# First attention stage: the weights in memory with all heads of a token and key side by side, and pairs of heads 8 apart

## The reference

```python
disp = (x @ w_disp + b_disp)            # 16 heads of 16
val  = (x @ w_val + b_val)              # 16 heads of 16
val_win = windows(val, 32)              # for each token the 32 tokens that end with it
logits = bond(disp windows) - 10 * damage(disp windows)   # two GELUs of [b, head, t, 32, 16]
weights = softmax(where(cmask, logits, -inf), axis=-1)    # over the 32 keys
out = einsum('bntd,bntde->bnte', weights, val_win)
return out.transpose(0, 2, 1, 3).reshape(B, T, C) @ w_cproj + b_cproj
```

## Time and profile before

| | |
|---|---|
| median of three runs | 3115.01 us |
| lowest and highest | 3107.58 and 3115.89 us |
| the profiled execution | 3107.8 us |
| its span, first to last instruction | 3106.1 us |
| mean granted TensorE clock | 0.951 |
| busy in the span: PE, DVE, ACT, POOL | 91%, 54%, 50%, 42% |
| first attention, some 600 to 1330 us, in the stretch 820 to 880: PE, DVE, ACT, POOL busy | 53.1, 49.8, 53.4, 50.1 of 60 us |

### The profile page before, as it was taken

The page is one execution under the profiler, slowest core; times in us unless marked ns, Lnnn a source line. Parts: engine busy times, 40 slices in busy tenths (PEclk is TensorE's granted clock), DMA queues, the critical chain, the costliest instruction groups (busy, mean ns, idle before and its releaser), DMA issues. The chain is left out here.

```text
span 3106.1 us, 54232 instructions
## 1 busy us (share of the span) xinstructions
PE 2824.6 (91%) x19419; PEld 2032.8 (65%) x19419; DVE 1674.6 (54%) x4656; ACT 1556.4 (50%) x2621; POOL 1317.7 (42%) x1315
## 2 busy tenths in 40 slices
PE   6899999877898988588999998999879999998999
PEld 5799999732444443368999996666546566655676
DVE  5411111288888888363111112677776666666666
ACT  1133333369899898311333332333257777783333
POOL 5444444379888888163444442000043443320000
PEclk9899999889999999768999998999989999999999
DMA  8299999705566555862999997000052333301000
GB/s 288 73 327 328 325 329 325 224 16 37 59 60 65 56 62 62 97 201 86 326 325 328 328 326 228 5 1 1 25 133 72 78 98 94 91 1 39 14 14 20
DMA packets 360543, 432.23 MB, mean 139 GB/s; under 512 B 86721, under 2 KB 315238, under 8 KB 357222
## 3 DMA queue, kind: packets, MB, share of 16 engines
q1 hardware_dynamic: 334902, 394.66, 48.0%
q0 software_dynamic: 24576, 33.57, 5.1%
q10 hardware_dynamic: 816, 0.79, 0.1%
HBM read 356.08 MB, written 72.88 MB: 138 GB/s over the span
## 5 line engine op out<-in xcount | busy, mean ns | idle before, releaser
L1806 ACT ACTIVATE f_h_t<-f_h_ps,f_b_t 128x128 f32<-128x128 f32 x1024 | 319.6, 363 | 596.3 <-PE f_h_ps L1764 596.0
L2186 POOL TENSOR_TENSOR a_dmg_buf<-a_c 128x2048 f32<-128x2048 f32 x128 | 519.9, 4096 | 77.8 <-PE a_dmg_ps L2250 48.4
L1764 PEld LDWEIGHTS f_h_ps<-f_rows_t,f_w 128*128 128x128 f32 x4096 | 482.8, 194 | 9.9 <-issue 3.5
L1764 PE MATMUL f_h_ps<-f_rows_t,f_w 128*128 128x128 f32 x4096 | 483.9, 277 | 2.3 <-DVE f_rows_t L1820 1.2
L1778 PE MATMUL f_y_ps<-f_w,f_h_t 128*128 128x256 f32 x2048 | 483.4, 379 | 0.0
L1724 POOL DMA_INDIRECT acc_rows<-f_y,f_give x128 | 205.0, 1602 | 487.6 <-DMA acc_rows<-f_y,f_give 441.1
L1778 PEld LDWEIGHTS f_y_ps<-f_w,f_h_t 128*128 128x128 f32 x2048 | 369.8, 190 | 39.9
L1820 DVE COPY f_rows_t<-f_t_ps 128x256 f32<-128x256 f32 x128 | 54.3, 424 | 597.9 <-PE f_t_ps L1752 597.9
L2562 DVE SCALAR_TENSOR_TENSOR a_bond_buf<-a_a,a_small_rep,a_q_ps 128x512 f32<-128x512 f32 x512 | 346.6, 739 | 8.0 <-PE a_q_ps L2380 4.2
L999 ACT ACTIVATE a_prob<-a_prob,a_neg_top 128x384 f32<-128x384 f32 (+3 forms) x512 | 276.5, 570 | 46.7 <-POOL a_neg_top L816 46.5
L536 DVE SCALAR_TENSOR_TENSOR x_resid<-f_y_ps,f_gate,x_resid 128x256 f32 x512 | 216.7, 478 | 122.5 <-PE f_y_ps L384 111.9
(11 more groups left out here) (358 smaller groups left out, 4135.4 us busy)
## 6 DMA issues: line engine op xcount, KB each, us to landing
f_w<-in_L_ffn_w_dram SPq DMA_DIRECT2D x256, 1024.0 KB
a_skewed<-skew SPq DMA_DIRECT2D x32, 512.0 KB, 6.8
a_k_s<-parts SPq DMA_DIRECT2D x16, 768.0 KB, 7.8
acc_rows<-x_resid SPq DMA_DIRECT2D x17, 512.0 KB, 7.8
xn_rows<-f_xn SPq DMA_DIRECT2D x16, 512.0 KB, 3.6
a_vals<-val_rows SPq DMA_DIRECT2D x64, 128.0 KB, 3.9
skew<-a_bond SPq DMA_DIRECT2D x128, 64.0 KB
x_resid<-acc_rows SPq DMA_DIRECT2D x30, 256.0 KB, 7.0
```

The lines of the kernel that those rows point to most:

```text
L1764: last = nc.tensor.matmul(h_ps[n // HB][:, (n % HB) * P:(n % HB + 1) * P], w1_sb[s][:, c, n * P:(n + 1) * P], rows_t[e % 2][:, c, :], star ...
L1806: nc.scalar.activation(h_t[k][:, n, :], h_ps[n // HB][:, (n % HB) * P:(n % HB + 1) * P], ACT.Gelu, bias=b1_t[:, n, e:e + 1]).then_inc(gelu ...
L2186: nc.gpsimd.tensor_tensor(dmg_buf[n % RING][:, :, :], places(c_sb[h], first_place(dg)), c_sb[h][:, PAD:].unsqueeze(1).broadcast_to([P, DG, ...
```

## The change

The weights of a token are kept with the head as the innermost axis: `bond` becomes [128, 4 tiles, 32 keys, 16 heads], and `skew` and `skewed` are keys x heads as well. A token's 512 weights of a tile are then one run of 2 KB in SBUF and in DRAM, and a row is shifted by one key, 16 elements, against the row before. The 16 stores and 4 loads stay as they are in number and bytes. `copy_logits` writes in the new order, `find_top` and `inverse_sums` reduce over an axis whose elements are 16 apart, `less_top` subtracts along the middle axis. A block for `turn_weights` is now every eighth column, `skewed[:, x, hp::8]`, which holds heads hp and hp + 8, alternating, for 64 keys. So `vals` has its two halves on alternating partitions, the sums go to two places 128 columns apart in the result, and the values come out of their product in their natural order: `w_val` and `b_val` are used unsorted, and the copy of the bias to `b_val_r` goes.

```diff
--- before.py
+++ after.py
@@ -1892,7 +1892,7 @@
         sb = lambda n, s, dt=FP32: ctx.enter_context(nc.sbuf_tensor(f"{name}_{n}", s, dt))
         ps = lambda n, s: ctx.enter_context(nc.psum_tensor(f"{name}_{n}", s, FP32))
         sem = lambda n: core.semaphore(f"{name}_{n}")
-        w_val_sb = sb("w_val", [P, DC, HP, 2, BD])
+        w_val_sb = sb("w_val", [P, DC, D])
         w_out_sb = sb("w_out", [P, DC, D])
 
         b_out_sb = sb("b_out", [3, D])
@@ -1901,8 +1901,7 @@
         ones = sb("ones", [3, P], BF16)
         w_disp_sb = sb("w_disp", [P, DC, D])
         b_disp_r = sb("b_disp", [P, D])
-        b_val_sb = sb("b_val", [P, HP, 2, BD])
-        b_val_r = sb("b_val_r", [P, 2, HP, BD])
+        b_val_sb = sb("b_val", [P, D])
         bond_b = sb("bond_b", [P, 1])
         damage_b = sb("damage_b", [P, 1])
 
@@ -1948,8 +1947,9 @@
         dmg_buf = [sb(f"dmg_buf{k}", [P, DG, S]) for k in range(RING)]
         tanh = sb("tanh", [P, S])
         logits = sb("logits", [P, S])
-        bond = [sb(f"bond{k}", [P, TPB, NH, WIN]) for k in range(2)]
-        top = sb("top", [P, TPB * NH, 1])
+
+        bond = [sb(f"bond{k}", [P, TPB, WIN, NH]) for k in range(2)]
+        top = sb("top", [P, TPB, NH])
         inv_sum = [sb(f"inv_sum{k}", [P, TPB, NH]) for k in range(2)]
         skewed = sb("skewed", [P, TPB, NH * SPAN])
         turned = sb("turned", [P, HP, P])
@@ -2088,8 +2088,8 @@
                 sp.dma_start(dst, src, **kind).then_inc(loaded, 16)
             sp.dma_start(w_disp_sb[:, :, :], w_disp.rearrange("(c p) n -> p c n", p=P)).then_inc(disp_loaded, 16)
             load(b_disp_r[:, :], b_disp.partition_broadcast(P))
-            load(w_val_sb[:, :, :, :, :].rearrange("p c h r d -> p c (h r d)"), w_val.rearrange("(c p) n -> p c n", p=P))
-            load(b_val_sb[:, :, :, :].rearrange("p h r d -> p (h r d)"), b_val.partition_broadcast(P))
+            load(w_val_sb[:, :, :], w_val.rearrange("(c p) n -> p c n", p=P))
+            load(b_val_sb[:, :], b_val.partition_broadcast(P))
             load(bond_b[:, :], b_bond.partition_broadcast(P))
             load(damage_b[:, :], b_damage_out.partition_broadcast(P))
             load(w_out_sb[:, :, :], w_cproj.rearrange("(c p) n -> p c n", p=P))
@@ -2106,9 +2106,10 @@
                     if j:
                         sp.wait_ge(skew_loaded[x], j * 16)
                     for a in range(BPT):
-                        rows = bass.AP(tensor=skew_dram.tensor, offset=a * WIN * row + x * NH * SPAN + 1,
-                                       ap=[[row + 1, WIN], [SPAN, NH], [1, WIN]])
-                        sp.dma_start(rows, bond[j % 2][a * WIN:(a + 1) * WIN, x, :, :]).then_inc(skew_stored[x], 16)
+                        rows = bass.AP(tensor=skew_dram.tensor, offset=a * WIN * row + x * NH * SPAN + NH,
+                                       ap=[[row + NH, WIN], [1, WIN * NH]])
+                        sp.dma_start(rows, bond[j % 2][a * WIN:(a + 1) * WIN, x, :, :].rearrange("p w h -> p (w h)")
+                                     ).then_inc(skew_stored[x], 16)
                 for x in range(TPB):
                     if j:
                         sp.wait_ge(w_turned, (j - 1) * TPB + x + 1)
@@ -2135,7 +2136,7 @@
                 for r in range(2):
                     first = val_dram[S - WIN + x * P:, r * HP * BD:]
                     blocks = bass.AP(tensor=first.tensor, offset=first.offset, ap=[[D, SPAN], [WIN * D, BPT], [1, HP * BD]])
-                    sp.dma_start(vals[r * SPAN:(r + 1) * SPAN, x * BPT:(x + 1) * BPT, r, :], blocks).then_inc(val_loaded[x], 16)
+                    sp.dma_start(vals[r:2 * SPAN:2, x * BPT:(x + 1) * BPT, r, :], blocks).then_inc(val_loaded[x], 16)
 
             sp.wait_ge(core.cleared, 16 * core.clears)
             store_values(0)
@@ -2190,9 +2191,9 @@
             def less_top(j):
                 for n, tiles in enumerate(soft_parts(j)):
                     count = tiles.stop - tiles.start
-                    rows = bond[j % 2][:, tiles, :, :].rearrange("p j h w -> p (j h) w")
+                    rows = bond[j % 2][:, tiles, :, :]
                     pool.wait_ge(top_ready, j + n + 1)
-                    nc.gpsimd.tensor_tensor(rows, rows, top[:, tiles.start * NH:tiles.stop * NH, :].broadcast_to([P, count * NH, WIN]),
+                    nc.gpsimd.tensor_tensor(rows, rows, top[:, tiles, :].unsqueeze(2).broadcast_to([P, count, WIN, NH]),
                                             ALU.subtract).then_inc(soft_ready, 1)
 
             def split_bias():
@@ -2274,7 +2275,7 @@
                 for hp in range(HP):
                     bank = (t_ps, second(m))[hp // 4]
                     last = nc.tensor.transpose(bank[:, hp % 4 * P:(hp % 4 + 1) * P],
-                                               skewed[:, x, hp * P:(hp + 1) * P], core.ident[:, :])
+                                               skewed[:, x, hp:NH * SPAN:HP], core.ident[:, :])
                 last.then_inc(w_turned, 1)
 
             def sums(m):
@@ -2288,7 +2289,7 @@
                     pe.wait_ge(ctx_ready, m)
                 for hp in range(HP):
                     for a in range(BPT):
-                        last = nc.tensor.matmul(o_ps[a * WIN:(a + 1) * WIN, hp * 2 * BD:(hp + 1) * 2 * BD],
+                        last = nc.tensor.matmul(o_ps[a * WIN:(a + 1) * WIN, 0:D].rearrange("p (r h d) -> p h r d", r=2, d=BD)[:, hp, :, :],
                                                 turned[:, hp, a * WIN:(a + 1) * WIN],
                                                 vals[:, x * BPT + a, :, hp * BD:(hp + 1) * BD],
                                                 start=True, stop=True)
@@ -2308,7 +2309,7 @@
                     at = PAD + (2 * pair + j) * P
                     for c in range(DC):
                         last = nc.tensor.matmul(t_ps[:, j * D:(j + 1) * D], xn_t[i % NX][:, c, at:at + P],
-                                                w_val_sb[:, c, :, :, :].rearrange("p h r d -> p r h d"),
+                                                w_val_sb[:, c, :],
                                                 start=c == 0, stop=c == DC - 1)
                 last.then_inc(val_ready, 1)
 
@@ -2578,14 +2579,14 @@
 
                 j, part = divmod(g, GROUPS)
                 h, at = part // 2, slice(part % 2 * PG, (part % 2 + 1) * PG)
-                turned_g = bond_ps[g % 2][:, :].rearrange("p (j d h) -> p j h d", j=TPB, d=PG)
-                dst = bond[j % 2][:, :, h * HH:(h + 1) * HH, at]
+                turned_g = bond_ps[g % 2][:, :].rearrange("p (j d h) -> p j d h", j=TPB, d=PG)
+                dst = bond[j % 2][:, :, at, h * HH:(h + 1) * HH]
                 dve.wait_ge(logits_turned, g + 1)
                 if part == 0 and j >= 2:
                     for stored in skew_stored:
                         dve.wait_ge(stored, (j - 1) * 16 * BPT)
                 nc.vector.scalar_tensor_tensor(out=dst[:, 0, :, :], in0=turned_g[:, 0, :, :], scalar=bond_b[:, 0:1],
-                                               in1=early[:, at].unsqueeze(1).broadcast_to([P, HH, PG]),
+                                               in1=early[:, at].unsqueeze(2).broadcast_to([P, PG, HH]),
                                                op0=ALU.add, op1=ALU.add)
                 nc.vector.tensor_scalar(dst[:, 1:, :, :], turned_g[:, 1:, :, :], bond_b[:, 0:1], None,
                                         ALU.add).then_inc(logits_copied, 1)
@@ -2595,14 +2596,13 @@
                     dve.wait_ge(soft_ready, j)
                 nc.vector.drain()
                 for tiles in soft_parts(j):
-                    nc.vector.tensor_reduce(top[:, tiles.start * NH:tiles.stop * NH, 0],
-                                            bond[j % 2][:, tiles, :, :].rearrange("p j h w -> p (j h) w"),
+                    nc.vector.tensor_reduce(top[:, tiles, :], bond[j % 2][:, tiles, :, :].rearrange("p j w h -> p j h w"),
                                             AX.X, ALU.max).then_inc(top_ready, 1)
 
             def inverse_sums(j):
                 dve.wait_ge(exp_done, j + len(soft_parts(j)))
-                nc.vector.tensor_reduce(inv_sum[j % 2][:, :, :].rearrange("p j h -> p (j h)"),
-                                        bond[j % 2][:, :, :, :].rearrange("p j h w -> p (j h) w"), AX.X, ALU.add)
+                nc.vector.tensor_reduce(inv_sum[j % 2][:, :, :], bond[j % 2][:, :, :, :].rearrange("p j w h -> p j h w"),
+                                        AX.X, ALU.add)
                 nc.vector.drain()
                 nc.vector.reciprocal(inv_sum[j % 2][:, :, :], inv_sum[j % 2][:, :, :])
 
@@ -2631,7 +2631,7 @@
                 nc.vector.tensor_tensor(
                     val_rows[:, 2 * pair:2 * pair + 2, :, :].rearrange("p j r n -> p j (r n)"),
                     t_ps[:, :].rearrange("p (j n) -> p j n", j=2),
-                    b_val_r[:, :, :, :].rearrange("p r h d -> p (r h d)").unsqueeze(1).broadcast_to([P, 2, D]),
```

(2 more changed lines are left out.)

## The result

| kernel | median us | span of the profiled execution |
|---|---|---|
| before, 5 runs (3100.4 to 3115.9) | 3107.58 | 3106.1 |
| changed, 5 runs (3079.9 to 3082.4) | 3081.56 | 3078.1 |

The ratio is 0.992, with a 95% interval from 0.9899 to 0.9941: some 26 us faster. In a later session the same two kernels stood at 0.9947 (0.9930 to 0.9964), 16 us.

A forecast was written before the change was run, and what follows sets the result against it. No single bound for the program; in the first attention stage ScalarE sets the pace outside the ends. Gains of 27.9 us less 5.3 (reductions) and 5.9 (weight loads) leave 16.7, so 3115.0 becomes 3098.3 us, range 3083 to 3120.

The forecast's parts named there:

- a faster transfer brings nothing: Batches 1 to 5: ScalarE waits 1.57 and 0.72 us at two tiles with the load already in; zero gain claimed.
- nothing that shows: Start of the stage: removing the one copy of `b_val_r` was claimed to give no visible gain.
- The tail, 18.5 us: Last batch's end: stores issue in 6.9 us, the load lands before TensorE is free, all 18.5 us come back.
- The waits of 5.3 and 4.1 us: ScalarE's waits in batches 0 and 6, claimed to vanish because loads come 13.6 us earlier.
- small pieces: Stores of 64 KB: 512 pieces of 128 B become 32 of 2 KB, so 16 take 6.9 us, not 20.48.
- The fifth rival: Stores aren't limited by their pieces: no gain, only the cost of 11.2 us, 3126.2 us; chance 0.03.
- The price of a step, 0.37 ns: Both VectorE reductions: stepped reads cost 0.37 ns an element more, 0.76 us each, taken from a small reduction stepping 16 B.
- the first rival: Steps cost ScalarE's 0.86 ns an element: 31.4 us of costs against 27.9 of gains, 3118.5 us; chance 0.20.
- `find_top` covered by 0.79 us: After `find_top` the chunk is ready 0.79 us before ScalarE wants it, so 0.76 us more costs nothing.
- Weight loads, 5.9 us: Transposes of `turn_weights`: stepped loads cost 0.052 us each, the middle of two bounds, 0.42 a tile at 14 tiles.
- `less_top`, not priced: GpSimd's subtraction after `find_top`: only its wait for the longer reduction was considered, covered by two further steps; no own cost.
- The base: Starting time from which the gain was subtracted: 3115.0 us, the median of the runs shown (3107.6 to 3115.9).

## Why the prediction missed, step by step

The time came out below the range although the costs were twice the forecast. What failed is what the sum put at nothing: the gain in batches 1 to 5, "a faster transfer brings nothing", which is 13.8 us, and the copy taken away, "nothing that shows", behind which lie 9.7. In the profiled executions the forecast's span is 3106.1 - 16.7 = 3089.4 us and the measured one 3078.1, 11.3 less: 17.2 more gained in the stage, 9.7 gained behind it, 12.7 more paid for the steps and 2.9 lost ahead of the stage. Between the medians the base adds to it.

- **The tail, 18.5 us: right in size, by luck in part.** The next stage starts 18.3 us earlier after the first store. The stores took 8.5 and not 6.9 us, and the first load was issued at 8.6 us. The forecast had the load landed before TensorE is free; it was the other way round: TensorE was free 10.9 us after the first store in place of 14.5, as the pause of 3.8 us had gone, and waited 3.4 us for the load. The pause and the wait cancel.
- **The waits of 5.3 and 4.1 us: gone,** as forecast; batch 0 is 6.5 us shorter, batch 6 only 2.2, because the steps took their part.
- **Its reason, small pieces: wrong.** The range was built on issuing against pieces; what decided was where they begin. The fifth rival (not limited by pieces) was nearly right in its premise and wrong in its time.
- **The price of a step, 0.37 ns: wrong.** It is (3732 - 2286) / 2048 = 0.71 ns, nearer ScalarE's 0.86 than the small reduction's 0.37, whose step was four times shorter. It lies near the first rival's price.
- **`find_top` covered by 0.79 us: the worst of the costs.** It costs 8.6 us. I had looked at one chunk behind it; VectorE stays late through the steps that follow, and `inverse_sums` then adds to the same lateness. Forecast for both 5.3, measured 20.2. This error worked against the two above.
- **Weight loads, 5.9 us: too high.** Their duration rose from about 150 to 196 ns, but they start 0.11 us apart as before, and no time could be measured for them. The middle of two bounds was no estimate: the loads overlap.
- **`less_top`, not priced:** 0.9 us longer each, 1.6 us of the stage.
- **Batches 1 to 5, "a faster transfer brings nothing": the step that failed.** With aligned pieces they take 382.2 us in place of 396.0, a gain of 13.8 (13.1 by the second trace of before). I had looked only at the waits for the turned weights, which did stay at 1.6 and 0.7 us. The gain lies in VectorE's gaps of 0.7 to 2.7 us behind the sums, which the slow stores cause, and in a granted clock of 0.94 to 0.98 where it is 0.98 to 1.00 afterwards; by what means the stores act on either stays open. In the changed kernel itself the five batches take 401.1 us, 5.1 more than before: the steps cost more there than this gain.
- **Behind the stage, "nothing that shows" for the copy: wrong,** 9.7 us in the first traces, 6.1 in the second, of which the pauses in the loop are 5 to 6.
- **The base.** 3115.0 was the median of three; with five it was 3107.6, and 3098 to 3106 in the later sessions. That alone is 7.4 us of the 16.7 by which the result of 3081.6 lies below the forecast of 3098.3.

So costs of 24 us in place of 11.2 and gains of some 45 in the stage in place of 27.9 (615.4 to 570.3, all reads in order; 35 from the second trace of before), with 6 to 10 behind it: the errors went against each other, and the net gain, 16.7 forecast, was 26 and, by the repeated measurement, 16. That the second agrees with the forecast is luck.

## What to carry to other kernels

Before pieces are made larger, look at whether they begin at a multiple of 64 B: one run with all pieces moved onto it tells size from place. Price a longer instruction on an engine that works back to back by the whole stretch until it next waits, not by the slack of its next consumer; and if it is late, first try to put half of the work a few steps off. And a gain that lies outside the code that was changed should be tested with one instruction put in or taken out before it is believed.

## What was not expected of the hardware

- 128 B pieces written 4 B off a multiple of 64 B: 24 to 26 us for 1 MB in 16 stores, against 10.7 to 12.3 at multiples of 64 B.
- While such slow stores are under way, VectorE starts 0.7 to 2.9 us after the end of the products that it waits for, against 0.03 to 0.05 us with aligned pieces, and TensorE pauses for 1.9 to 3.8 us in the middle of 64 products.
- A reduction on VectorE with a step of 64 B in SBUF: 0.71 ns an element more; `copy_logits`, which read PSUM with a step of 32 B before and in order after (its writes changed too), takes 607 and 609 ns.
- One VectorE instruction more at the start of the stage: 15 more packets of instructions and 9 to 10 us, more than 700 us behind it.
- VectorE with both operands in SBUF beside a busy GpSimd: 0.69 or 4.84 us for the same 512 elements.
